# A three-layer feature-crossing tower: the order of a chunk's steps, the pairs that are split, the layout of x_pair

## The reference, cut to what matters

```python
for i in range(3):                       # B = 512, E = 16; G = 32, 64, 64
    z = (x0[:, :, None, :] * h[:, None, :, :]).reshape(B, F * G, E)
    y = relu(einsum('oc,bce->boe', W[i], z) + b[i])
    if i != 2:
        keep, h = y[:, :64], y[:, 64:]
    else:
        keep = y
out = sum(concat(keeps), axis=2)         # then three dense layers on top
```

## Time and profile before

| | |
|---|---|
| runs | 542.85, 543.13, 1859.66 us; median 543.13 |
| profiled execution | 546.4 us, span 544.6 us |
| mean granted TensorE clock | 0.984 |
| busy | PE 501.3 us (92%), DVE 379.8 (70%), POOL 358.2 (66%), ACT 196.1 (36%) |

### The profile page before, as it was taken

The page is one execution under the profiler, slowest core; times in us unless marked ns, Lnnn a source line. Parts: engine busy times, 40 slices in busy tenths (PEclk is TensorE's granted clock), DMA queues, the critical chain, the costliest instruction groups (busy, mean ns, idle before and its releaser), DMA issues.

```text
span 544.6 us, 4268 instructions
## 1 busy us (share of the span) xinstructions
PE 501.3 (92%) x1446; PEld 273.1 (50%) x1446; DVE 379.8 (70%) x219; ACT 196.1 (36%) x253; POOL 358.2 (66%) x220
## 2 busy tenths in 40 slices
PE   0966769899999999999999999999999989899987
PEld 0622335355555555555545555555555554455555
DVE  1333964695959595959687786959595969867573
ACT  1210340434434443534253434334444424241242
POOL 5770347597969697887969696969697744715000
PEclk9897997999999999999999999999999999999999
DMA  7679599349998989797979797979798777350200
GB/s 230 131 164 255 150 243 233 105 110 250 219 247 184 250 182 238 167 235 160 228 158 231 166 227 161 221 166 243 159 220 199 171 196 159 89 110 9 76 0 0
DMA packets 33549, 94.50 MB, mean 174 GB/s; under 512 B 7844, under 2 KB 15012, under 8 KB 25080
## 3 DMA queue, kind: packets, MB, share of 16 engines
q1 hardware_dynamic: 27208, 91.87, 70.7%
q0 software_dynamic: 4096, 1.06, 1.7%
q10 hardware_dynamic: 2224, 1.31, 1.2%
HBM read 92.05 MB, written 2.10 MB: 173 GB/s over the span
## 4 chain that ended last, share of the span: by engine, by line
PE 75%; DVE 10%; issue 5%; DMA 4%; POOL 3%; ACT 2%; SPq 0%; DVEq 0%; ACTq 0%
PE acc L624 26%; PE acc L637 15%; PE spare L624 14%; PE x_bank L624 12%; DVE z L434 7%; PE x_bank L637 3%; POOL gathered L369 3%; PE spare L637 3%; DMA gathered<-in_table,rows_all 2%; DMA x_pair<-x_scratch 2%; DVE z L422 1%; DVE zl_parts L446 1%; DVE sum L451 1%; PE acc L642 1%; ACT h L534 1%
## 5 line engine op out<-in xcount | busy, mean ns | idle before, releaser
L382 POOL TENSOR_TENSOR z_low<-z,z_high 128x1024 fp32r<-128x1024 f32 x88 | 214.4, 2447 | 110.2 <-ACT z_high L520 109.4
L434 DVE TENSOR_TENSOR z<-h,x_pair 128x2048 f32<-128x2048 f32 (+1 forms) x65 | 144.8, 2248 | 115.8 <-ACT h L534 105.6
L624 PE MATMUL acc<-z,w_direct 128*128 128x512 f32 x384 | 175.0, 598 | 11.1 <-DVE z L434 11.1
L369 POOL DMA_INDIRECT gathered<-in_table,rows_all x128 | 143.6, 1122 | 33.3 <-issue 26.4
L520 ACT ACTIVATE z_high<-z 128x1024 fp32r<-128x1024 f32 x90 | 93.3, 1054 | 149.7 <-DVE z L434 127.7
L624 PEld LDWEIGHTS acc<-z,w_direct 128*128 128x128 f32 x384 | 72.9, 191 | 91.1 <-issue 71.9
L624 PE MATMUL spare<-z,w_direct 128*128 128x512 f32 x200 | 92.9, 603 | 11.2 <-DVE z L434 11.2
L624 PE MATMUL x_bank<-z,w_direct 128*128 128x512 f32 x200 | 89.9, 593 | 4.6 <-DVE z L434 4.6
L434 DVE TENSOR_TENSOR z<-h_odd,x_pair 128x2048 f32<-128x2048 f32 x32 | 72.3, 2278 | 8.1 <-ACT h_odd L534 8.1
L434 DVE TENSOR_TENSOR z<-h_even,x_pair 128x2048 f32<-128x2048 f32 (+1 forms) x33 | 72.3, 2213 | 5.2 <-ACT h_even L534 5.2
L624 PEld LDWEIGHTS spare<-z,w_direct 128*128 128x128 f32 x200 | 38.1, 193 | 55.6 <-issue 41.7
(11 more groups left out here) (144 smaller groups left out, 273.0 us busy)
## 6 DMA issues: line engine op xcount, KB each, us to landing
x_pair<-x_scratch SPq DMA_DIRECT2D x126, 512.0 KB, 7.2
x_rot<-x_scratch SPq DMA_DIRECT2D x60, 256.0 KB, 5.3
x_rep<-x_scratch SPq DMA_DIRECT2D x15, 256.0 KB, 5.1
w_direct<-in_W SPq DMA_DIRECT2D x2, 1024.0 KB, 8.6
gathered<-in_table,rows_all POOLq DMA_INDIRECT x128, 8.0
x_scratch<-gathered SPq DMA_DIRECT2D x32, 64.0 KB, 1.6
x_pair<-x_scratch ACTq DMA_DIRECT2D x2, 512.0 KB, 8.0
x_pair<-in_W_top SPq DMA_DIRECT2D x2, 512.0 KB
```

The costliest lines, as they stand in the source:

```text
L369: pool.indirect_dma_start(gathered[:, c % X_SLOTS, j, :], None, table, bass.IndirectOffsetOnAxis(ap=rows.bitcast(U32), axis=0),).then_inc( ...
L382: nc.gpsimd.tensor_tensor(z_low[:, slot_of(pair)], products_of(pair), z_high[:, slot_of(pair)].bitcast(F32), ALU.subtract).then_inc(low_po ...
L434: nc.vector.tensor_tensor(z[:, step.group % Z_SLOTS, first:end], h[:].unsqueeze(1).to_broadcast([P, end - first, N]), x_pair[:, chunk % 2, ...
L624: op = nc.tensor.matmul(bank_of(pair)[:], w_direct[:, first + i], products_of(pair)[:, i], start=i == 0 and pair is OPENS[pair.layer, pair ...
```

## The change

The list of steps, `TURN`, is written anew. A turn of chunk c now has: layer 1 of c, k = 0, 1, 2; layer 0 of c+1; layer 1 of c, k = 3; layer 2 of chunk c-1, k = 2 and 3; layer 2 of c, k = 0 and 1. `SPLIT` has six pairs in place of four: the pair i = 1 of k = 0, 1, 2 in both layers. Of the eight split pairs of a turn VectorE makes `z_low` for four (`BY_VECTOR`), GpSimd for the other four. In `x_pair` the four tiles of a step no longer lie side by side in a partition but four tiles apart. At the start all four steps' `x_pair` of chunk 0 are loaded by SyncE and ScalarE together, before chunk 1 is stored, and the first matmuls have 128 partitions in place of 32, the rest zero. Twice 22 transposes are put before the first steps of layers 1 and 2 (`keep_warm`), and 30 stand where 28 stood.

```diff
-TURN = ((1, 0), (2, 0), (1, 1), (2, 1), (0, 0), (1, 2), (1, 3), (2, 2), (2, 3))
-OF = {0: 1, 1: 0, 2: -1}
-FIRST = ([(1, 0, k) for k in range(GROUPS)] + [(2, 0, 0), (2, 0, 1), (0, 1, 0), (2, 0, 2), (2, 0, 3)]
-         + [(1, 1, 0), (0, 2, 0)] + [(1, 1, k) for k in range(1, GROUPS)])
-SPLIT = ((1, 0, 1), (1, 1, 1), (2, 1, 1), (2, 2, 1))
+TURN = ((1, 0, 0), (1, 0, 1), (1, 0, 2), (0, 1, 0), (1, 0, 3), (2, -1, 2), (2, -1, 3), (2, 0, 0), (2, 0, 1))
+FIRST = [(1, 0, k) for k in range(GROUPS)] + [(0, 1, 0), (2, 0, 0), (2, 0, 1)]
+SPLIT = ((1, 0, 1), (1, 1, 1), (1, 2, 1), (2, 0, 1), (2, 1, 1), (2, 2, 1))
+BY_VECTOR = ((0, 0, 1), (1, 1, 1), (2, 0, 1), (2, 1, 1))
 def hands(layer, chunk, k):
-    low = "vector" if (layer, chunk) == (2, CHUNKS - 1) else "pool"
-    return tuple(low if chunk and (layer, k, i) in AT else "tensor" for i in range(2))
+    def by(of):
+        if not chunk or of not in AT:
+            return "tensor"
+        return "vector" if of in BY_VECTOR or (layer, chunk) == (2, CHUNKS - 1) else "pool"
...
-SUM01, SUM2 = 1, 4
+SUM01, SUM2 = 1, 6
 def outputs():
-    at = {(0, c): PLACE[1, c, 0] for c in range(CHUNKS)}
-    at |= {(1, c): PLACE[2, c - 1, GROUPS - 1] if c >= 2 else PLACE[2, c, 0] for c in range(CHUNKS)}
-    at |= {(2, c): PLACE[2, c + 1, 0] if c else PLACE[1, 1, 1] for c in range(CHUNKS - 1)}
+    at = {(0, c): PLACE[2, c - 1, 0] if c >= 2 else PLACE[1, c, 0] for c in range(CHUNKS)}
+    at |= {(1, c): PLACE[2, c - 1, GROUPS - 1] if c else PLACE[2, 0, 0] for c in range(CHUNKS)}
+    at |= {(2, c): PLACE[1, c + 2, 2] if c + 2 < CHUNKS else PLACE[2, c + 1, 2] for c in range(CHUNKS - 1)}
...
-        x_pair = sb("x_pair", [P, 2, TILES, N])
+        x_pair = sb("x_pair", [P, 2, GROUP, GROUPS, N])
...
             sp.wait_ge(x_stored[0], 32)
-            for k in range(2):
+            for k in range(GROUPS):
                 load_half(sp, 0, k, 0)
             store_x(sp, 1)
-            for k in range(2, GROUPS):
-                load_pair(0, k)
...
+                if step in HALVED:
+                    keep_warm(banks[step.layer][0], WARM)
```

More of the change, by code:

```diff
@@ L23 @@
 X0_LOADS, SMALL, TOPS = GROUP + 1, 2, COPIES + 2
-BUSY = 28
+BUSY, WARM = 30, 22
 AHEAD = 3
@@ L96, in plan @@
     start = step(0, 0, 0)
-    order = FIRST + [(layer, c + OF[layer], k) for c in range(2, CHUNKS + 1) for layer, k in TURN
-                     if c + OF[layer] < CHUNKS]
+    order = FIRST + [(layer, c + offset, k) for c in range(1, CHUNKS + 1) for layer, offset, k in TURN
+                     if c + offset < CHUNKS]
     return start, [step(*of) for of in order]
@@ L146 @@
 CLOSES = {(pair.layer, pair.chunk): pair for pair in ORDER}
-LAST1 = max((pair for step in PLAN for pair in step.by("pool") if step.layer < 2), key=lambda pair: pair.split)
-LAST_SLOT = max((pair for step in PLAN for pair in step.by("pool") if pair.split % PAIR_SLOTS == PAIR_SLOTS - 1),
+LAST1 = max((pair for step in PLAN for pair in step.by("vector", "pool") if step.layer < 2),
+            key=lambda pair: pair.split)
+LAST_SLOT = max((pair for step in PLAN for pair in step.by("vector", "pool") if pair.split % PAIR_SLOTS == 0),
                 key=lambda pair: pair.split)
@@ L215, in dlrm_tower @@
         w_sym = z[:, 3].rearrange("p t n -> p (t n)")[:, 0:GROUP * P].rearrange("p (t o) -> p t o", o=P)
[L218 to L227, removed]
+        x_first = x_rot[:, 0, :]
+        sel = x_rot[:, 1:3].rearrange("p t n -> p (t n)")[:, 0:X0_LOADS * P].rearrange("p (t o) -> p t o", o=P)
+        free = x_pair[:, 0].rearrange("p i k n -> p (i k) n")
+        result = free[0:1, 0, :]
+        hid2 = free[:, 4:6, :]
+        wt1 = free[:, 6:8, :]
+        wt2 = flat(free[:, 8:10, :])
+        wd = free[0:COPIES * DENSE, 10, :]
+        wt1_high, wt1_low = z_high[:, 0], z_low[:, 0]
         wt2_high, wt2_low = [flat(w[:, 0:2 * N // P]) for w in (w_high, w_low)]
         sum01_high, sum01_low = zl_high[:], zl_parts[:]
-        sum2_high, sum2_low = z_high[:, 0, 0], z_low[:, 0, 0]
-        hid1_high, hid1_low = [parts[:, 1:3].rearrange("p s i n -> p (s i) n") for parts in (z_high, z_low)]
+        sum2_high, sum2_low = z_high[:, 1, 0], z_low[:, 1, 0]
+        hid1_high, hid1_low = [parts[:, 2:4].rearrange("p s i n -> p (s i) n") for parts in (z_high, z_low)]
         acc = [psum("acc0"), psum("acc1"), psum("acc2")]
@@ L361, in _ @@
             sp.wait_ge(result_ready, 1)
-            sp.dma_start(out.rearrange("b o -> o b"), result[:]).then_inc(out_stored, 16)
+            sp.dma_start(out.rearrange("b o -> o b"), result).then_inc(out_stored, 16)
             sp.wait_ge(out_stored, 16)
@@ L435, in products @@
                                             h[:].unsqueeze(1).to_broadcast([P, end - first, N]),
-                                            x_pair[:, chunk % 2, GROUP * k + first:GROUP * k + end, :],
+                                            x_pair[:, chunk % 2, first:end, k, :],
                                             ALU.mult).then_inc(z_made if end == GROUP else first_made, 1)
@@ L478, in _ @@
                         sum_components(chunk, kept01[:, chunk % 2], sum01, kept_out[1], sum01_made)
-                    if n == PLACE[2, chunk, GROUPS - 1] + SUM2:
+                    if chunk < CHUNKS - 1 and n == min(PLACE[2, chunk, GROUPS - 1] + SUM2, len(PLAN) - 1):
                         sum_components(chunk, kept2[:], sum2, kept_out[2], sum2_made)
@@ L654, in spread_first, with keep_warm @@
                     nc.tensor.matmul(bank[:], sel[:, j], x_first, start=True, stop=True).then_inc(spread, 1)
+            def keep_warm(bank, count):
+                for _ in range(count):
+                    nc.tensor.transpose(bank[:, 0:P], ident[:], ident[:])
             def start():
@@ L675, in _ @@
             turn_dense()
-            for _ in range(BUSY):
-                nc.tensor.transpose(acc[0][:, 0:P], ident[:], ident[:])
+            keep_warm(acc[0], BUSY)
             spread_first()
@@ L729 @@
     takes = np.concatenate([np.arange(FIELDS).repeat(GROUP).reshape(1, P), near.reshape(GROUP, P) % FIELDS])
-    sel = (np.arange(FIELDS)[:, None, None] == takes).astype(np.float32)
+    sel = (np.arange(P)[:, None, None] == takes).astype(np.float32)
     signs = np.zeros((P, 4), np.float32)
```

14 lines of the change are left out of this document (8 added, 6 removed).

## The result

The changed kernel takes **570.37 us** (median of four runs, 569.1 to 571.76); the kernel before, over the same comparison, 545.31. (One of its four runs took 1859.66 us and is left out of the ratio.) The ratio is **1.047, 95% interval 1.043 to 1.050**: slower. The forecast was 566 us, 4.2% slower. The profiled execution took 570.6 us, its span 568.8, where the sum said 567.2.

What follows compares the result with a forecast made beforehand. TensorE bound the old steady part; after the change, a loop through all engines would. Start 87.5 + 13 x 31.5 + end 62.2 = 559.2 us, plus 8.0 for the clock = 567.2, given as 566 us; range 545 to 583.

Steps and rivals of the forecast that it cites:

- The loop, 31.5 us: Steady turn through ScalarE, VectorE and TensorE: 29.4 us of waits and work, plus 2.1 us for the exclusion.
- Step 1: ScalarE after C: layer 0's outputs, then the rounding for layer 2's k = 0, and on to VectorE, 3.2 us.
- C: End of layer 0's last matmul of a chunk, where the loop starts and closes; C(2) is chunk 2's, forecast at 87.5 us.
- Step 2: VectorE's list from the waiting `z_low` to layer 1's product k = 3: 16.35 us, before 2.1 for the exclusion.
- Step 3: TensorE from layer 1's product k = 3 through its pairs and layer 0 to the next C: 9.8 us.
- The point of decision: Whether `zl_parts` goes from 0.74 to 2.8 us, with layer 0's product and POOL asking 0.1 us apart.
- the exclusion does not bite: Rival: POOL asks later than `zl_parts`; 29.4 us a turn, no clock falls, 530 us, 2.4% faster; chance 0.12.
- The clock: TensorE's clock falls after one idle in three, 1.85 us each over 13 turns: 8 us, bounds 0 and 24.
- three idles of this size: TensorE's idles before the old kernel's steady part, one followed by a clock fall, taken as the one-in-three share.
- The start: Chunk 0's loads through chunk 1's turn: C of chunk 1 at 59.4 us, of chunk 2 at 87.5.
- TensorE stays full: Rival: ScalarE's rounding comes sooner, loop under 28.47 us; 517 us, 4.8% faster; chance 0.07.
- The second clash: Rival: a new VectorE `z_low` falls behind POOL's subtraction, up to 2.4 us more a turn, 597 us; chance 0.08.

Runs made afterwards that it cites:

- e5: e3 with layer 0's second `z_low` made by POOL in place of VectorE: 28.46 us a turn, ratio 0.954 to the kernel before.
- e6: Changed kernel with layer 1's k = 3 ahead of layer 0's step and layer 0's split pairs one step behind it: 28.49 us a turn, ratio 0.955.
- e1: Changed kernel with one added wait, POOL's subtraction for layer 1, k = 2 behind `zl_parts`: 29.22 us a turn, ratio 0.976.
- e2: Changed kernel with ScalarE's rounding for layer 2, k = 0 ahead of layer 0's outputs: 29.47 us a turn, ratio 0.979.
- r_after: The changed kernel, unedited, run again on a later chip: 31.37 us a turn, 584.9 us, ratio 1.040 to the kernel before.
- e4: Changed kernel with 20 transposes ahead of layer 1's k = 3 in each turn: 31.37 us a turn, ratio 1.027.
- e7: Changed kernel with the old layout of `x_pair`, a step's four tiles side by side: 31.37 us a turn, 586.0 us, ratio 1.042.
- e10: Changed kernel without the twice 22 transposes (`WARM` 22 to 0): 31.37 us a turn, 569.6 us, ratio 1.046.
- e3: Changed kernel with both the edits of e1 and e2: 29.83 us a turn, ratio 0.981.
- e9: Changed kernel with the new order but the old four split pairs and every `z_low` on POOL: 29.11 us a turn, ratio 0.970.

## Why the prediction was right

Point by point, by its own steps.

- *TensorE's turn of 28.47 us when full.* Measured 28.46 and 28.49 in e5 and e6. The prices of a pair from the earlier trace rows hold.
- *The loop, 31.5 us.* Measured 31.37. Step 1, C to the first `z_low`: 3.01 us (281.96 to 284.97), booked 3.2. Step 2 with the exclusion, 284.97 to 303.46: 18.5, booked 16.35 + 2.1. Step 3, 272.14 to 281.94 in the turn ahead: 9.8, booked 9.8. Shown by taking away: 2.15 us for the exclusion (e1), 1.9 for the rounding (e2).
- *Who asks first.* Booked 0.1 us between the two; measured 0.12, in the same order in all 13 turns. The point of decision was as near as it had seemed. e1 is the rival "the exclusion does not bite": 29.22 us a turn, where it said 29.4.
- *TensorE's idle, 2.8 us, ended by product k = 3.* 2.64 us.
- *The clock.* Here luck had a large part. Booked were 8.0 us for one fall in three; measured were five falls in 13 turns, four of 1.7 us and one of 2.9, 9.7 in all (six and 10.2 in r_after). But the "three idles of this size" were not that: the one with the fall went from 38.83 (31.72 + 7.11) to 44.51, 5.7 us, twice the others. Of the two idles of 2.83 us neither was followed by a fall, so the rows gave no share for idles of that size, and the one that was booked happened to be near 5 of 13. That the falls hang on the idle is shown by e4.
- *The start.* Here the sizes were off. C of chunk 1 came at 63.2 us, booked 59.4; its first product at 64.65, booked 60.9. The data of layer 0 of chunk 1, booked for 45.7, let its product start at 47.30, 1.6 us late: the store of chunk 1, which those loads wait for, took 7.4 us to land behind the loads of `x_pair`, where before the change it took 1.6. And the first matmuls of layer 2 ran at the lower clock (5.72 us for eight records, booked 3.7), 2.0 us for which I had booked nothing, leaning on the transposes. 1.6 + 2.0 makes nearly all of the 3.8. The working has a slip there too: 4.2 MB at 213 GB/s from 18.9 end at 38.6, not 39.5; the last of these loads let product k = 3 start at 39.02. C(2) was late by 1.6 us only (89.1 against 87.5), since the turn of chunk 1 was shorter than the full loop.
- *The end.* 568.8 - 506.63 = 62.2 us, booked 62.2.
- *The sum.* 89.1 + 417.5 (13 turns and the falls; booked 409.5 + 8.0) + 62.2 = 568.8. The turns by themselves are 13 x 31.37 = 407.8, 1.7 under the booking, and the falls 9.7, 1.7 over it. The last step, 3.3 us down to the median of before, was wrong: the profiled execution was no slower than the others (570.6 against 570.4), and without that step the forecast would have been 569. By the same sums the rival "TensorE stays full" is at 518 us, not 517.
- *Edits booked at nothing.* Layout (e7) and keep_warm (e10): nothing that shows.
- *The second clash.* It happens in small in the changed kernel, a `z_low` of 1.58 us at 303.38 beside a subtraction, off the loop; in e3 it is whole, 2.6 us.

What the prediction didn't see is what the change was worth: the order was good but for one place, the place of layer 0's step. Moving it behind k = 3 (and its split pairs one step up), with the same pairs and the same hands, turned 4.0% slower into 4.5% faster on one chip (r_after and e6); e5 got there with other hands.

## What to carry to other kernels

When an instruction is moved, walk the loop through all engines' lists once, with the waits; busy sums said that VectorE had room (26.2 of 28.5 us), and it had none where it was needed. Where VectorE's instructions with two SBUF operands and POOL's exclude each other, put an instruction with a PSUM operand beside POOL's, by order or by an added wait, and look where POOL's next one falls. Take the gain apart before giving a change up: here one part was worth 16 us, and the loss of the other went with an edit of two lines.

## What the runs showed of the hardware

- The exclusion takes in GpSimd's gathers, and it doubles up: VectorE's request that falls on a gather waits for it and for POOL's next subtraction too. In e9 layer 0's product, asked at 298.46, takes 5.11 us in place of 2.28, and POOL's next gather, asked at 301.56 beside it, 2.83 in place of 0.95:

```profile
298.07 0.95 POOL L379 DMA_INDIRECT gathered<-in_table,row  x1
298.46 5.11 DVE L433 TENSOR_TENSOR z<-x_rep,x_rot 128x2048 f32<-128x2048 f32 x1
299.05 2.35 POOL L392 TENSOR_TENSOR z_low<-z,z_high 128x1024 fp32r<-128x1024 f32 x1
301.56 2.83 POOL L379 DMA_INDIRECT gathered<-in_table,row  x1 [0.16 <-issue]
```

  The Trainium skill, "SBUF — State Buffer" (Who interferes with whom), has the order of issue decide who is blocked; with these rows the engine that is served next can be the one that just held it.
- On two chips of four the kernels take 15 to 20 us longer, for the changed kernel all of it ahead of C(2), where ScalarE, and in e6 VectorE too, stands still behind the loads of `x_pair` with no releaser that a row names. The cause stays open.
- Transposes in an idle of 2.6 us kept the clock in all of e4's turns; 22 of them ahead of an idle of 6.3 us did not. Without them, equal idles of 2.64 us were followed by a fall in some turns (4 of 12 in the first run, 5 of 12 in r_after) and not in others.
